# One batch's opening steps in another order on TensorE, ScalarE and VectorE, in a two-layer cross-attention kernel

## What is computed

```python
def layer(emb, latent, Wq, bq, Wk, bk, Wv, bv, gamma, beta):
    q = einsum('bte,ef->btf', emb, Wq) + bq
    k = einsum('bml,le->bme', latent, Wk) + bk
    v = einsum('bml,le->bme', latent, Wv) + bv
    w = softmax(einsum('bte,bme->btm', q, k) / sqrt(512), axis=1)   # over t
    x = einsum('btm,bme->bte', w, v) + emb
    mu, var = mean(x, -1), var(x, -1)
    return (x - mu) * rsqrt(var + 1e-6) * gamma + beta

x = layer(x, ctx_512, *L0)     # x: 32 x 224 x 512, ctx_512: 32 x 750 x 256
x = layer(x, ctx_512, *L1)
```

## Time and profile before

| | |
|---|---|
| median of 3 runs | 978.75 us (978.2 to 979.07) |
| the profiled execution | 978.5 us, of which the span of its instructions is 976.7 us |
| TensorE busy | 960.5 us, 98% of the span |
| VectorE, ScalarE, GpSimd busy | 866.2, 739.4, 711.2 us |
| granted TensorE clock, mean | 0.998 of full speed |

### The profile page before, as it was taken

The page is one execution under the profiler, slowest core; times in us unless marked ns, Lnnn a source line. Parts: engine busy times, 40 slices in busy tenths (PEclk is TensorE's granted clock), DMA queues, the critical chain, the costliest instruction groups (busy, mean ns, idle before and its releaser), DMA issues.

```text
span 976.7 us, 25194 instructions
## 1 busy us (share of the span) xinstructions
PE 960.5 (98%) x7180; PEld 908.5 (93%) x7180; DVE 866.2 (89%) x2602; ACT 739.4 (76%) x2068; POOL 711.2 (73%) x649
## 2 busy tenths in 40 slices
PE   7999999999999999999999999999999999999996
PEld 6889999999999999999999999999999999999986
DVE  4889899999898989999999999999989899999867
ACT  3657877777887787887787887777788778788764
POOL 0346787778777777878777878777877777787874
PEclk9999999999999999999999999999999999999999
DMA  7754444554443554344455444455444355434101
GB/s 223 167 103 92 105 102 89 114 113 85 107 104 81 110 117 99 88 104 93 98 117 105 87 105 98 91 111 111 87 104 101 83 111 119 98 91 105 42 22 47
DMA packets 362872, 98.35 MB, mean 101 GB/s; under 512 B 308648, under 2 KB 346696, under 8 KB 362824
## 3 DMA queue, kind: packets, MB, share of 16 engines
q1 hardware_dynamic: 360280, 96.98, 45.1%
q10 hardware_dynamic: 2544, 0.80, 0.4%
HBM read 83.06 MB, written 14.68 MB: 100 GB/s over the span
## 4 chain that ended last, share of the span: by engine, by line
PE 96%; DVE 1%; ACT 1%; DMA 1%; issue 1%; SPq 0%; DVEq 0%; ACTq 0%
PE oq_bank L780 14%; PE score_bank L739 9%; PE score_bank L744 9%; PE score_bank L740 8%; PE pv_bank L815 6%; PE pv_bank L817 6%; PE pv_bank L824 6%; PE oq_bank L716 6%; PE oq_bank L711 6%; PE oq_bank L712 6%; PE oq_bank L775 4%; PE oq_bank L776 4%; PE oq_bank L784 4%; PE t_bank L668 2%; PE oq_bank L791 1%; PE t_bank L690 1%
## 5 line engine op out<-in xcount | busy, mean ns | idle before, releaser
L1061 ACT ACTIVATE probs<-probs,neg_max 125x224 f32<-125x224 f32 x378 | 178.0, 473 | 82.5 <-DVE neg_max L1495 81.7
L739 PE MATMUL score_bank<-qT_hi,cT_hi 128*125 128x224 f32 x768 | 197.1, 283 | 1.1 <-ACT qT_hi L1053 0.6
L740 PE MATMUL score_bank<-qT_hi,cT_lo 128*125 128x224 f32 x768 | 188.4, 271 | 0.0
L1897 POOL TENSOR_TENSOR p_lo<-probs,p_hi 125x672 fp32r<-125x672 f32 x60 | 98.4, 1639 | 95.0 <-DVE p_hi L1531 95.0
L780 PE MATMUL oq_bank<-probs,raw 125*128 125x224 f32 x720 | 156.8, 354 | 0.0
L1083 ACT ACTIVATE probs<-probs,rsum 125x224 f32<-125x224 f32 x378 | 150.9, 473 | 1.4 <-DVE rsum L1515 1.4
L739 PEld LDWEIGHTS score_bank<-qT_hi,cT_hi 128*125 128x125 f32 x768 | 144.9, 189 | 2.7 <-ACT qT_hi L1053 1.3
L744 PE MATMUL score_bank<-qT_lo,cT_hi 128*125 128x224 f32 x768 | 147.2, 273 | 0.0
L1995 POOL TENSOR_TENSOR y_out<-z,gamma_row 112x512 f32<-112x512 f32 x60 | 77.1, 1309 | 94.0 <-ACT z L1128 94.0
L1495 DVE CUSTOM_DVE_ANT_0 probs<-score_bank,d_row 125x224 f32<-125x224 f32 x384 | 138.4, 380 | 8.0 <-PE score_bank L744 4.5
L740 PEld LDWEIGHTS score_bank<-qT_hi,cT_lo 128*125 128x125 f32 x768 | 145.0, 189 | 0.0
(11 more groups left out here) (169 smaller groups left out, 2754.5 us busy)
## 6 DMA issues: line engine op xcount, KB each, us to landing
cb<-in_ctx_dram SPq DMA_DIRECT2D x248, 92.0 KB
x<-in_x_dram SPq DMA_DIRECT2D x32, 448.0 KB, 4.0
xb<-in_x_dram SPq DMA_DIRECT2D x124, 112.0 KB, 2.7
out_dram<-y_out SPq DMA_DIRECT2D x31, 448.0 KB, 5.0
raw<-in_ctx_dram SPq DMA_DIRECT2D x32, 375.0 KB
raw<-in_ctx_dram SPq DMA_DIRECT2D x64, 187.5 KB
cb<-in_ctx_dram SPq DMA_DIRECT2D x124, 3.5 KB
y<-in_L_xattn_Wq_dram SPq DMA_DIRECT2D x2, 512.0 KB, 5.2
```

Source lines behind the costliest of these rows:

```text
L739: nc.tensor.matmul(o, cT_hi[:, u.slot, l, cols], qT_hi[:, l, :], start=(l == 0), stop=False)
L740: nc.tensor.matmul(o, cT_lo[:, u.slot, l, cols], qT_hi[:, l, :], start=False, stop=False)
L1061: ins = act.activation(probs[0:MP, u.par4, c, :], probs[0:MP, u.par4, c, :], ACT.Exp, bias=neg_max[0:MP, u.par4, c:c + 1], scale=-1.0, acc ...
```

## The change

Only calls in the opening lists move. On TensorE `spread_d(a1)` comes behind the first score pair of a1 and no longer behind the second. On ScalarE the first half of a1's `normalise` comes ahead of `xT_hi_part(b0, 1)` and `exps(a1, 1)`. On VectorE `invert_sum(a1, 0)` comes ahead of the last two maxima, and `turn_x(a2, 0)` behind `xT_lo_part(b0, 1)`. No instruction is added or taken away, and nothing moves on GpSimd or in the transfers.

```diff
--- before.py
+++ after.py
@@ -894,8 +894,8 @@
                 q_product(a1, 0)
                 q_product(a1, 1)
                 score_product(a1, 0)
+                spread_d(a1)
                 score_product(a1, 1)
-                spread_d(a1)
                 fold_w(1)
                 spread_bq(1)
                 transpose_x(b0, 0)
@@ -1239,10 +1239,10 @@
             take_w(1)
             xT_hi_part(b0, 0)
             exps(a1, 0)
+            normalise(a1, 0)
             xT_hi_part(b0, 1)
             exps(a1, 1)
             q_hi(b0, 0)
-            normalise(a1, 0)
             normalise(a1, 1)
             q_hi(b0, 1)
             xT_hi_part(a2, 0)
@@ -1782,12 +1782,12 @@
                 score_max(a1, c)
             fold_c(1, 0)
             xT_lo_part(b0, 0)
+            invert_sum(a1, 0)
             score_max(a1, 4)
             score_max(a1, 5)
-            invert_sum(a1, 0)
-            turn_x(a2, 0)
             fold_c(1, 1)
             xT_lo_part(b0, 1)
+            turn_x(a2, 0)
             invert_sum(a1, 1)
             fold_c(1, 2)
             q_lo(b0, 0)
```

## The result

| | before | changed |
|---|---|---|
| median of 9 runs each | 978.75 us (978.09 to 980.99) | 980.95 us (980.17 to 982.67) |
| span of the profiled execution | 976.7 us | 978.8 us |
| granted TensorE clock, mean | 0.998 | 0.998 |

The account below looks back on a forecast made before the run. TensorE never waits in the turns, so lateness in the opening reaches the end: 0.37 + 0.24 + 1.12 - 0.64 - 0.24 + 1.19 + 0.27 = 2.31 us on 978.75, forecast as 981.0 us, range 979.2 to 982.0.

Parts of the forecast that it names:

- The turns pass a loss on one for one, and the path through VectorE and ScalarE decides: Opening's VectorE and ScalarE path sets o_product(b0, 0), where TensorE waits 0.80 us; lateness there reaches the end in full.
- The spread's new wait, 0.37: TensorE at spread_d(a1): a1's second dot takes 1.22 us, d comes at 52.32, so the spread waits 0.37 us.
- The first rival: Dots of b0 not held: 0.85 us late, 0.48 if a1's dot is short too; held less, 1.33; chance 0.27.
- The early d is worth nothing to the exponentials: ScalarE: exps(a1, 0) stands behind xT_hi_part(b0, 0), so moves from 55.51 to 55.88 although d_row comes 0.94 us earlier.
- 0.24 + 1.12 - 0.64: ScalarE before xT_hi_part(b0, 1): 0.24 us wait for the inversion, 1.12 for three multiplications, less 0.64 of former idle time.
- The 0.24 that VectorE had to spare: VectorE at q_lo(b0, 1): q_hi(b0, 1), which it waited for, comes earlier, so 0.24 us of lateness is saved.
- The dots, 1.19 and 0.27: Dots of b0 on VectorE stand until GpSimd's sum_thirds and sum_two end, then need 0.55: 1.19 and 0.27 us more.
- The sum: At q_lo(b0, 1) and everything behind it on the path: all terms together make 2.31 us late.
- The clock: Rival: TensorE's clock falls to 1.2 GHz for 3.6 us during new opening waits, costing 1.8 more: 982.8 us; chance 0.04.
- The faster case: Rival: normalise hidden in ScalarE's idle 0.64 and early d passed on remove TensorE's waits: 977.6 or 976.8 us; chance 0.04.

Follow-up runs that it names:

- run 7a: Kernel before with one ScalarE swap, o_hi(a1, 0) ahead of xT_hi_part(a2, 1): 978.21 us beside 978.82, ratio 0.9995.
- run 3: Changed kernel with GpSimd's sum_thirds(a1) waiting for both dots of b0: 979.6 us beside 978.94 of before, ratio 1.0012.
- run 8: Changed kernel with GpSimd's scale(a0, 0) waiting for the dots of a1 and sum_thirds(a1) for those of b0: 979.04 us beside 978.82 of before, ratio 1.0004.
- run 1: Kernel before with only spread_d(a1) moved ahead of the second score pair: 978.98 us beside 978.94, ratio 0.9997.
- run 2: Kernel before with only normalise(a1, 0) and invert_sum(a1, 0) moved as in the change: 980.68 us beside 978.94, ratio 1.0018.
- run 6: Kernel before with a GpSimd copy of 125 x 672 added ahead of sum_thirds(a1), under the dots of b0: 978.67 us beside 978.82.
- run 4: Kernel before with a GpSimd addition on 125 x 672 added ahead of sum_thirds(a1): 981.48 us beside 978.94, ratio 1.0026.
- run 5: Kernel before with a GpSimd fill of 125 x 672 with zero added ahead of sum_thirds(a1): 978.71 us beside 978.82.

## Why the prediction held

- **The turns pass a loss on one for one, and the path through VectorE and ScalarE decides.** Held: 380.00 of 380.00 us busy in the turns, and run 7a, which shortened the path on ScalarE alone. The last wait tells the same: it is 0.80 before and in the changed kernel, and 0.60 and 0.61 in runs 3 and 8, the changed kernel with short dots of b0. In run 8 TensorE comes to that wait 0.67 later than before and the path only 0.48, so the wait is shorter, but it is still the path that TensorE waits for.
- **The spread's new wait, 0.37.** The mechanism held, the size did not: in the profile of the change the second dot of a1 takes 0.73, the spread waits for nothing, and the term is 0. In run 3 the dot took 1.20 and the path is 0.32 longer than in run 8; in run 1 it took 1.81 and TensorE waited 0.71. I had explained the 1.22 us by the add_beta that it started under, and yet took it over as if the changed kernel would meet the same add_beta at the same point. That differs from execution to execution. The first rival had this case (d ready at 51.92, no wait, an order that costs 0.48), and the profile of the change bears out that half of it; the other half, dots of b0 that are not held, failed.
- **The early d is worth nothing to the exponentials.** Held in the changed kernel: d_row comes early and exps(a1, 0) starts at 55.59, behind xT_hi_part(b0, 0), in place of 55.51. In a kernel whose normalise stays in its old place it does bring 0.29, since the third score pair and the second transposes come earlier; that gain is gone with the early normalise, for the order costs 0.48 with the early spread (run 8) and 1.86 - 1.13 - 0.27 = 0.46 without it (run 2).
- **0.24 + 1.12 - 0.64.** Held: the wait is 0.24, the three multiplications hold ScalarE from 57.33 to 58.46, and from the start of the path to xT_hi_part(b0, 1) it is 7.64 us where it was 6.89, 0.75 more; with the 0.37 off, 0.72 was forecast.
- **The 0.24 that VectorE had to spare** at q_lo(b0, 1). Held, and seen alone in run 6. The sentence that VectorE never has anything to spare on the path was not right here.
- **The dots, 1.19 and 0.27.** Measured 1.13 and 0.27. sum_thirds started 0.29 ahead of the dot (0.26 forecast) and took 1.61, not 1.64. The step that I was least sure of, a hold longer than the 0.67 us that any row had shown, held to 1.51 us in run 4. The Trainium skill (GPSIMD Engine Reference, Key points) names contention on shared SBUF interfaces for VectorE's instructions with two SBUF inputs; the traces agree for the dots under additions and under the copy, but not under the fill of run 5, and the sizes are theirs. That fold_c, with one operand in a bank, is not hit shows in the kernel before: a fold_c(1, 0) that started with 0.75 us of a subtraction on GpSimd left took 0.68, and the next one, free of GpSimd, 0.67 (GpSimd, then VectorE):

```profile
55.37 1.01 POOL L1909 TENSOR_TENSOR raw_lo<-raw,raw_hi 125x384 fp32r<-125x384 f32 x1
```

```profile
55.63 0.68 DVE L1373 CUSTOM_DVE_ANT_0 dot_junk<-Wk_next,pv_bank 128x512 f32<-128x512 f32 x1
...
58.22 0.67 DVE L1373 CUSTOM_DVE_ANT_0 dot_junk<-Wk_next,pv_bank 128x512 f32<-128x512 f32 x1
```

- **The sum.** 2.31 forecast, of which the profile has 2.31 - 0.37 + 0.03 - 0.06 = 1.91, and the path measures 1.89. The median moved by 2.20; it is no sharper than 1.5 to 3.1 us by its interval, and how often the spread's 0.37 was in the runs stays open. That 981.0 came so close to 980.95 is luck: in the profile the term of 0.37 was 0, and without it the same sum gives 980.7. The range of 979.2 to 982.0 was wide enough for either.
- **The rivals.** The clock stayed: the mean granted clock is 0.998 in both, and 1.00 from 44 to 82 us, with waits of 1.32 and 1.04 us. The 3.6 us of low clock that I put into its price is not what the end shows: from about 972.4 to the end of the span at 976.7 it is 4.3. The faster case failed where it was said to: the exponentials started at 55.59. A wait that I did not name, 0.58 us in front of L824, is the same lateness seen one step earlier on TensorE, and adds nothing.

## What to carry to other kernels

An order written out by hand on strict engines has to be judged by the path that it feeds, not by the wait that it removes: the first normalise ran 3 us earlier, and nobody had been waiting for it. Where GpSimd works beside VectorE, ask of every reorder which of VectorE's instructions with two operands in SBUF will then start under a GpSimd instruction; an addition of 1.6 us on GpSimd cost one dot 1.1 us here, and 1.3 in run 4, and a wait on GpSimd, which had the time, gives it back. Edits worth half a us can be compared on one stretch of the trace between two marks when the times of whole runs can't tell them apart.

## What the runs showed of the hardware that was not expected

- A dot (112 x 512, two operands in SBUF) that starts under a GpSimd addition or copy ends 0.55 us behind it, to 0.01 us in the five cases of this text with 0.60 to 1.51 us left. It is so in the turns as well: in the profile of before, 29 dots between 80 and 976 us start under a scale with 0.24 to 0.43 us left, and each ends 0.54 to 0.56 behind it (0.79 to 0.98 us in place of 0.75). TensorE is busy throughout all the same in the stretch shown, 120 to 500 us.
- Under a fill of 125 x 672 the dot stays at 0.74. So it is GpSimd's reading that counts, and one operand is enough; fill and copy are one case each.
- It works the other way too: sum_two takes 0.66 us alone and 0.99 where it was issued under a dot, ending 0.52 behind the dot. sum_thirds, 1.61 and 1.62 alone (runs 8 and 3), took 2.06 in run 4 under a held dot, and 2.06 in run 6 under one of 0.75 that nothing held; it ended 1.47 and 1.48 behind the dot.
- The second dot of a1 took 0.73 to 1.81 us in the eleven profiles, by what GpSimd was doing when it started, though nothing ahead of it on VectorE was moved. Where d is spread early, TensorE waited for it (0.71 us in run 1); how much that makes the time vary from run to run was not measured.
